# One tile of empty rows doubled in DRAM, routed pads out of the first message steps, normalised rows a step later, tile table turned by a product

## The reference

```python
h = layernorm(x)                                   # 6250 x 256
msg = silu(concat(h[src], h[dst], w) @ mW1 + mb1)  # per edge
msg = silu((layernorm(msg) * g + b) @ mW2 + mb2)
agg = segment_sum(msg, src)
x = x + h + silu(concat(h, agg) @ uW1 + ub1) @ uW2 + ub2
t = layernorm(x)
p = softmax(t @ router_w.T); top two of 8, weights made to sum to 1
x = x + t + sum over the two of weight * (gelu(t @ w1[e] + b1[e]) @ w2[e] + b2[e])
```

## Time and profile before

| | us |
|---|---|
| median of 3 runs (2641.22 to 2647.70) | 2642.83 |
| profiled execution | 2642.2 |
| its span | 2640.4 |
| TensorE busy | 2384.5 (90%) |
| weight loads busy | 2048.0 (78%) |
| DVE busy | 2008.8 (76%) |
| ACT busy | 1718.9 (65%) |
| Pool busy | 1346.7 (51%) |

### The profile page before, as it was taken

How to read it: one execution, slowest core, us unless ns; L and a number is a source line. 1 busy time by engine, 2 the same in 40 slices (tenths; PEclk the granted TensorE clock), 3 DMA queues, 4 the chain that set the end, 5 groups by cost and what they waited for, 6 DMA issues and landing times. The chain is left out here.

```text
span 2640.4 us, 61405 instructions
## 1 busy us (share of the span) xinstructions
PE 2384.5 (90%) x15222; PEld 2048.0 (78%) x15223; DVE 2008.8 (76%) x6272; ACT 1718.9 (65%) x5992; POOL 1346.7 (51%) x1343
## 2 busy tenths in 40 slices
PE   4199999879999999999999999999999988519997
PEld 4188888658888888888888888888888877518886
DVE  7899999567777777777777777777777757746653
ACT  0877777657777777777777777777777646623432
POOL 2047777555555555555555555555555312447666
PEclk7599999989999999999999999999999998759998
DMA  8001111253333333333333333333335663356775
GB/s 183 17 28 33 29 35 33 73 143 106 99 106 99 105 99 106 99 106 100 105 100 104 101 102 103 102 102 101 105 100 104 61 193 92 130 146 201 209 124 65
DMA packets 154617, 267.37 MB, mean 101 GB/s; under 512 B 35393, under 2 KB 103584, under 8 KB 152405
## 3 DMA queue, kind: packets, MB, share of 16 engines
q0 software_dynamic: 64656, 147.39, 21.7%
q1 hardware_dynamic: 89855, 118.71, 16.9%
HBM read 214.03 MB, written 75.13 MB: 110 GB/s over the span
## 5 line engine op out<-in xcount | busy, mean ns | idle before, releaser
L1083 POOL DMA_INDIRECT work<-dst_half,stage_i x848 | 809.8, 955 | 763.5 <-PE ps L1291 585.9
L1274 PE MATMUL ps<-W2c,work 128*128 128x256 f32 x3392 | 802.3, 379 | 0.0
L1274 PEld LDWEIGHTS ps<-W2c,work 128*128 128x128 f32 x3392 | 612.0, 190 | 70.7
L1109 DVE TENSOR_TENSOR agg<-agg,ps 125x256 f32 x848 | 352.8, 416 | 253.9 <-PE ps L1291 246.2
L1215 ACT ACTIVATE work<-ps 128x512 f32<-128x512 f32 x424 | 252.1, 595 | 351.4 <-PE ps L1291 351.3
L1291 PE MATMUL ps<-work 128*125 128x256 f32 x1696 | 435.2, 379 | 1.3 <-ACT work L1236 1.3
L1230 ACT ACTIVATE work<-work 128x256 f32<-128x256 f32 x848 | 341.1, 404 | 54.0 <-DVE work L1136 50.3
L1265 PE MATMUL ps<-ablk,work 128*128 x2544 | 351.1, 275 | 19.8 <-DVE work L1157 14.0
L1188 DVE SCALAR_TENSOR_TENSOR work<-ps,work,b2c 128x256 f32<-128x256 f32 x848 | 367.7, 474 | 0.0
L542 POOL DMA_INDIRECT edge_records<-stage,work x208 | 256.4, 1233 | 190.2 <-PE ps L969 126.4
L1222 ACT ACTIVATE work<-work 128x256 f32<-128x256 f32 x848 | 340.7, 406 | 0.3
(11 more groups left out here) (295 smaller groups left out, 3381.5 us busy)
## 6 DMA issues: line engine op xcount, KB each, us to landing
work<-tile_sources SPq DMA_DIRECT2D x106, 250.0 KB
first_choice_tokens<-pad_rows SPq DMA_DIRECT2D x106, 128.5 KB
work<-dst_half,stage_i POOLq DMA_INDIRECT x848, 2.8
work<-first_choice_tokens SPq DMA_DIRECT2D x28, 258.0 KB, 3.9
work<-second_choice_tokens SPq DMA_DIRECT2D x28, 258.0 KB, 3.1
work<-first_choice_tokens SPq DMA_DIRECT2D x28, 256.0 KB, 3.6
second_choice_tokens<-pad_rows SPq DMA_DIRECT2D x106, 64.5 KB
update_node_half<-work SPq DMA_DIRECT2D x25, 250.0 KB, 2.2
```

What stands on the lines that cost most here:

```text
L1083: pool.indirect_dma_start(bg[:, r, u, :], None, dstd, bass.IndirectOffsetOnAxis(ap=stage_i[:, c:c + 1], axis=0)).then_inc(gath[r], 16)
L1109: v.tensor_tensor(d, d, ps[0:NB, (7, 0)[a.mod(2)], u * D:(u + 1) * D], ALU.add).then_inc(agg_add, 1)
L1274: last = t_.matmul(ps[:, 5 + s, u * D:(u + 1) * D], sT[:, a.mod(RT), u, k], W2c[:, k], start=(k == 0), stop=(k == KC - 1))
```

## The change

1. `pad_rows` is made of one copy of 128 empty rows out of SBUF; three copies inside DRAM, each waited for, double it to 1024 rows.
2. The three tiles of pads at the end of the sort phase are gone, and the first six message steps lay none. These six tiles are laid in steps 96 to 101, one more pair of copies each.
3. In the update the finishing of the statistics stays at a lag of 5 (`UM`); the rows' normalising and transposes go to 6, the logits to 7.
4. Batches are 9, 8 and 8 pairs. `place` is cut: tiles per expert and the room left in one step, slots (`seat`) and the table of experts (`cover`) in the next; rows are routed from the step after, so one step later. There are six row buffers, and the working arrays lie past the table. For the last batch `cover` stands behind its sixth row.
5. The table of experts is turned by one product with the unit matrix (a column of 128 becomes a row), and DVE copies it, times 256, to where registers are loaded from.

```diff
-BATCHES = (9, 9, 7)
+BATCHES = (9, 8, 8)
...
                 sp.dma_start(uW1h, uW1[0:D, :].rearrange("(k p) n -> p k n", p=P)).then_inc(u_in, 16)
-                empty = rec[:, :, :].rearrange("p g f -> p (g f)")[:, 0:2 * XB]
-                for h in range(XD // 2):
-                    sp.dma_start(padd[2 * h * P:2 * (h + 1) * P, :].rearrange("(p d) w -> p (d w)", p=P),
-                                 empty).then_inc(zeros_out, 16)
+                sp.dma_start(padd[0:P, :], rec[:, :, :].rearrange("p g f -> p (g f)")[:, 0:XB]).then_inc(zeros_out, 16)
...
-                sp.wait_ge(zeros_out, 64 + 8 * XD)
+                sp.wait_ge(zeros_out, 80)
+                for h in range(3):
+                    n = P << h
+                    sp.dma_start(padd[n:2 * n, :], padd[0:n, :]).then_inc(pads_doubled, 16)
+                    sp.wait_ge(pads_doubled, 16 * (h + 1))
...
-                for g in range(TAILS // 2, XC):
-                    d = g % XD * P
-                    for k in range(K2):
-                        sp.dma_start(xsd[k][g * P:(g + 1) * P, :], padd[d:d + P, 0:(XW if k else XB)]).then_inc(xpads_out, 16)
...
-                dve.wait_ge(zeros_out, 64 + 8 * XD)
+                dve.wait_ge(zeros_out, 80)
...
-                        d = m.mod(2 * XD) * (P // 2)
-                        slots = bass.ds(m.of(P // 2), P // 2)
-                        for k in range(K2):
-                            sp.dma_start(xsd[k][slots, :], padd[d:d + P // 2, 0:(XW if k else XB)]).then_inc(xpads_out, 16)
+                        if not isinstance(m.it, int) or m.c >= SKIP:
+                            d = m.mod(2 * XD) * (P // 2)
+                            slots = bass.ds(m.of(P // 2), P // 2)
+                            for k in range(K2):
+                                sp.dma_start(xsd[k][slots, :], padd[d:d + P // 2, 0:(XW if k else XB)]).then_inc(xpads_out, 16)
+                        j = m.c - 12 * XD
+                        if isinstance(m.it, int) and 0 <= j < len(rest):
+                            g = rest[j]
+                            d = g % XD * P
+                            for k in range(K2):
+                                sp.dma_start(xsd[k][g * P:(g + 1) * P, :], padd[d:d + P, 0:(XW if k else XB)]).then_inc(xpads_out, 16)
+
+                    SKIP = 6
+                    rest = list(range(SKIP // 2)) + list(range(n_tails // 2, XC))
+                    assert n_tails - 12 * XD >= len(rest)
...
-        UA, U1, U2, UT, UL = 1, 2, 4, 5, 6
+        UA, U1, U2, UM, UT, UL = 1, 2, 4, 5, 6, 7
...
-        RS0 = 4
+        RS0 = 6
...
-        USTEPS = batches[-1][3] + 5
+        USTEPS = batches[-1][3] + 6
...
-                n = max(n, min(n + PACE[b] * max(m - first - 4, 0), t1))
+                n = max(n, min(n + PACE[b] * max(m - first - 5, 0), t1))
...
-                sp.wait_ge(xtab_ready, 1)
-                sp.dma_start(xtabd, xtabi).then_inc(xtab_out, 16)
-                sp.wait_ge(xtab_out, 16)
-                sp.dma_start(tabrow[0:1, PADT:PADT + P],
-                             xtabd.rearrange("p k -> (p k)").rearrange("(a n) -> a n", a=1)).then_inc(xtab_in, 16)
...
-                    a = m - UT
+                    a = m - UM
...
+                    link(v.scalar_tensor_tensor(out=xjumps[b % 2], in0=xtiles, scalar=1.0, in1=xjump, op0=ALU.min, op1=ALU.mult))
+                    link(v.scalar_tensor_tensor(out=xroom, in0=xtiles, scalar=float(P), in1=xover, op0=ALU.mult, op1=ALU.subtract))
+
+                def seat(b, t0, t1):
+
+                    w = t1 - t0
+                    tk_, sl_, pa_ = (by_expert(a, t0, t1) for a in (taken, slot, past))
                     link(v.scalar_tensor_tensor(out=xbase[n_], in0=ps[n_, 6, 0:XK], scalar=-1.0, in1=sl_[:, :, 0], op0=ALU.add, op1=ALU.subtract))
...
+                    link(v.tensor_tensor(xopen, xopen, ps[:, 7, 0:XK], ALU.add))
+                    link(v.tensor_tensor(xopen, xopen, xjumps[b % 2], ALU.add))
+
+                def cover(b):
                     for k in range(K2):
...
-                        link(v.tensor_reduce(out=xtab, in_=xcmp, axis=AX.X, op=ALU.add))
-                        v.tensor_scalar(xtabi, xtab, float(D), None, ALU.mult).then_inc(xtab_ready, 1)
-                        return
-                    link(v.scalar_tensor_tensor(out=xjump, in0=xtiles, scalar=1.0, in1=xjump, op0=ALU.min, op1=ALU.mult))
-                    link(v.tensor_tensor(xopen, xopen, ps[:, 7, 0:XK], ALU.add))
-                    link(v.tensor_tensor(xopen, xopen, xjump, ALU.add))
-                    link(v.scalar_tensor_tensor(out=xroom, in0=xtiles, scalar=float(P), in1=xover, op0=ALU.mult, op1=ALU.subtract))
+                        v.tensor_reduce(out=xtab, in_=xcmp, axis=AX.X, op=ALU.add).then_inc(xtab_ready, 1)
...
+                        if m == first + 4:
+                            seat(b, t0, t1)
+                            if b < len(batches) - 1:
+                                cover(b)
                     for t in range(routed(m), routed(m + 1)):
...
+                        if t == batches[-1][1] + RS0 - 1:
+                            cover(len(batches) - 1)
+                dve.wait_ge(xtab_ps, 1)
+                v.tensor_scalar(tabrow[0:1, PADT:PADT + P], ps[0:1, 6, P:2 * P], float(D), None, ALU.mult).then_inc(xtab_in, 16)
...
+                pe.wait_ge(xtab_ready, 1)
+                t_.matmul(ps[0:1, 6, P:2 * P], xtab, ident[:, :], start=True, stop=True).then_inc(xtab_ps, 1)
```

More of the change, by code:

```diff
@@ L1405, in routed @@
             for b, t0, t1, first in batches:
[L1406 removed]
+                n = max(n, min(n + PACE[b] * max(m - first - 5, 0), t1))
             return BK if m >= USTEPS else n
         ts0 = cut(RS0 * XB, "p (r w) -> p r w", r=RS0)
[L1410 to L1415 removed]
+        left = [past_tab + XK * TM * j for j in range(5)]
+        assert left[4] + 2 * P <= WORK
+        taken, slot, past, onex = (work[:, a:a + XK * TM] for a in left[0:4])
+        tri2, ones2 = (work[:, left[4] + P * j:left[4] + P * (j + 1)] for j in range(2))
         xcnt = cut(XK)
@@ L1428, in gnn_moe_kernel @@
         xtab = cut(1)
-        xtabi = cut(1, dt=i32)
+        xjumps = [cut(XK) for _ in range(2)]
         pidx = cut(K2)
```

19 lines of the change are left out of this document (6 added, 13 removed).

## The result

| | before | after |
|---|---|---|
| median, us | 2642.83 | 2630.41 (2626.62 to 2630.68) |
| profiled span | 2640.4 | 2628.5 |
| time of after over before, 95% interval | | 0.9945 (0.993 to 0.9959) |

The change is 0.55% faster: 12.4 us by the medians, 14.5 by the ratio. The forecast was 2622.6, 20.2 us under the median of before.

The account below looks back on a forecast made before the run. TensorE was taken as busy 9 tenths in most slices, the edits lying in its three holes. Terms -5.0, -3.5, -1.2, -3.3, -1.3, -1.0 and -4.3 sum to -19.6, so 2642.2 becomes 2622.6 us; range 2613 to 2632.

Parts of the forecast that it names:

- First copy: Start of the sort: fewer bytes of empty rows let DVE write its last table of ones earlier, -5.0 us.
- Doublings: Sort phase: three doubling copies on SP are covered by its wait before the first store, cost 0.
- Pads: Start of messages: -3.5 us, from SP's block ending 1.5 earlier and first tile rows landing 2.0 faster.
- Update, first steps: Start of the update: transposes a step later no longer make TensorE wait 1.81 us for rows, -1.2 us.
- Batch 0: Update, first batch's routing: TensorE's product restarts 4.6 us earlier, 1.3 lost to a slower product, -3.3 us.
- Batch 1: Update, second batch on DVE: 16 tiles instead of 18, one routed row and a wait less, -1.3 us.
- last batch: Update: table instructions moved behind the sixth row and six buffers, against one step more, -1.0 us.
- Burst: Pool's last scatters: 7.1 us stall gone, two rows more costing 2.5, -4.3 us.
- Rival 1: Last burst: the stall belongs to the scatters, not the table, so 7.1 us stay; 2629.7 us, chance 0.10.
- Rival 2: Update: lag and cut give nothing since DVE sets the pace, 6.8 us fewer gained; 2629.4 us, chance 0.10.
- Rival 3: Sort and message starts: both gains hidden by weights and gathers, 8.5 us back; 2631.1 us, chance 0.10.
- Rival 4: End of messages: late pads meet full DMA engines and TensorE waits 23 us for gathers; 2645.6 us, chance 0.04.

Follow-up runs that it names:

- e1: Kernel before with only the first edit: one copy of 128 empty rows, doubled three times inside DRAM; ratio 0.9982.
- e2: Kernel before with only the pads moved out of the sort's end and first six message steps into steps 96 to 101; ratio 0.9987.
- e9: The changed kernel run once more, unaltered, on another chip; ratio 0.9938 to the kernel before.
- e12: Changed kernel with batches of 9, 9 and 7, and seven unread products more on TensorE ahead of its waits around batches 0 and 1; ratio 0.9915.
- e3: Kernel before with only the table of experts turned by a product, without the write to DRAM; four row buffers kept; ratio 0.9973.
- e10: Kernel before with three edits together: the first copy, the pads and the table's product; ratio 0.9942.
- e11: Changed kernel with batches of 9, 10 and 6 and four rows a step for the second; median 2618.79 us, ratio 0.99 to the kernel before.
- e4: Kernel before with only the lag: normalised rows and transposes a step later, logits a step after that; ratio 0.9996.
- e5: Kernel before with only the long routing step cut in two and rows a step later, on a slower chip; ratio 0.9998.
- e6: Changed kernel with its table of experts written to DRAM and read back as before, on a slower chip; ratio 0.9941.

## Why the prediction was right, and where it was not

The time lies in the range and the direction is right; the sum of 19.6 came out as some 15.6 by the stretches on the usual chips (5.0 + 3.4 + 2.2 + 0.8 + 4.2), and as 12.4 to 16.4 by the times. The 4 us between lie in the update.

- First copy, -5.0: right, -4.8 by e1 and about 5 in the start of the last table. That only 2.2 us of it show at the last store of the two traces goes with TensorE's granted clock, which fell near 505 us in one and not in the other.
- Doublings, 0: right, 12.6 us under a cover of 57.
- Pads, -3.5: right, -3.4 by e2 and -3.7 in the stretch. Counted as the forecast did, from the end of the issue of the first rows to their use, it was 6.4 us before and is 4.7 in after, and 4.1 to 4.9 in e2 and e9 to e12; the forecast's -2.0 made it 4.4. None goes under the 3.9 us that the prediction estimated from the Trainium skill's rule on an outer dimension of 125, and none reaches it, so the runs neither show that floor nor speak against it.
- Update, first steps, -1.2: nothing in the two traces, 56.5 us from first to 13th load in both. The wait for the rows was taken by the one for DVE's sum. Over all traces the stretch is 55.6 to 58.5 us, so a gain of under 1 us is not shut out.
- Batch 0, -3.3: the restart right, what comes behind it not. The tenth product went 4.5 us earlier, where the forecast had 4.6. The step that failed is "1.3 back" for a slow product. What came back is 1.8 us at any clock, by a wait of TensorE for ACT's normalised rows in the next step (1.54 us in e12), which the prediction did not have. The slow products, 2.75 us in after, fill that wait and cost up to 1 us more. From the 13th to the 25th load 74.8 to 75.8 us (before, e1, e2, e3, e10) became 72.3 to 73.3 (after, e9, e11): -2.2 in the mean. And it needs lag and cut together: e4 has 75.1, e5 74.5.
- Batch 1, -1.3, and last batch, -1.0: together -0.8 (68.1 to 67.3 us from 25th load to burst). Batch 1's own four steps gave 1.0. The last batch gave nothing (33.4 and 33.5 us from there to the burst), and its term is the one that failed. The prediction left out how many rows of batch 1 DVE must put down, at Pool's 1.27 us each, before it can begin the last batch: nine in before and still nine with 9, 8, 8, and six when 9, 9, 7 stands in the changed kernel (e12). With the lag, the cut and six buffers e12 has 3.5 us less here, by nine rows becoming six.
- Burst, -4.3: right, -4.2, with both its parts: the stall gone (-6.8 in e3's burst), two rows more (+2.6). The prediction's own figures, 24.2 less 20.0, give 4.2.

The table's write, 512 bytes in words of 4, took 8.4 us from its issue to the read's before and 8.9 in e6. The rule of the Trainium skill, "DMA: Bandwidth & Descriptors", section "Anatomy of one DMA", is 2.0 us plus the bytes. That section measures DMAs that GpSimd issues, and this write was SP's; the measurement does not agree with the rule. The Trainium skill's line in the same page's "Specifications", that a transfer below 512 B becomes a read-modify-write, has no figure; that this is the reason for the 8.4 us no run here shows.

Rival 1 is out by e3 and e6. Rival 2 came to pass end to end: without lag, cut and 9, 8, 8 the time is the same (e10), and its 2629.4 is near the 2630.4 measured. Its reason holds in part. The waits for DVE's sum are there, but lag, cut and buffers gain 2.2 us up to the 25th load and 0.8 ahead of the burst, and 9, 8, 8 spends 2.6 on two rows more. By the later runs the gain is 16.4 us and not 12.4, so how near the time came to rival 2's is in part luck. Rival 3 is out by e1 and e2. Rival 4 did not come, at a DMA share of 0.99. What lag, cut and buffers are each worth beside 9, 9, 7 was not tried one by one: together, with seven products more, 13th load to last row is 152.6 us against 159.2 in e10.

## What to carry to other kernels

When several edits come in one change, price each by what the next engine in line does with it: here a shorter step on DVE was worth its length only if Pool, at a fixed 1.27 us a row, was not what DVE then waited for. A DMA of 512 bytes that takes one word from each of 128 partitions came with a stall of 7 us for the rows behind it; a product with the unit matrix does the same turn and the stall is gone. A product slowed by the clock costs its extra time only if nothing else waits in its step: 2.75 us of slow products cost 1 us here. And two traces in which TensorE's clock fell for a different time differed by 2 to 3 us in a stretch of 480, with and without the edit: compare a stretch over several traces before a gain is called lost.

## What was not expected of the hardware

- A stretch of the sort phase has two lengths, 476.2 to 476.9 us in three traces and 478.6 to 479.6 in seven. TensorE's granted clock stood at 0.50 for some 3 us of its end in the short ones and for some 7 or 10 in the long ones, behind a wait of 4.8 us or that and one of 2.1.
- One chip ran the same kernels 1.7% longer, with the message phase at its usual length (1523.4 us from the sixth use of tile rows to the first load of the update, in before as in e5): last table to last store 490 to 491 us and not 476 to 480, expert phase 308 to 317 and not 285. The cause was not looked for.
- Six pairs of pad copies, 386 KB a pair, late in the messages raised the DMA engines' share from 0.27 to 0.54 and cost nothing.
